# TensorE's slot reordered: transposition of x first, then the maximum, then the row, then projection and output matmuls

## Time and profile before

| what | value |
|---|---|
| median of 3 runs | 469.8 us (468.24 to 472.76) |
| the profiled execution, its own time | 469.28 us |
| its span, first to last instruction | 467.5 us |
| mean granted TensorE clock | 0.937 |
| busy: TensorE, its weight loads | 384.9 us (82%), 338.0 us (72%) |
| busy: VectorE, ScalarE, GpSimd | 380.4 us (81%), 358.4 us (77%), 295.8 us (63%) |

### The profile page before, as it was taken

The page is one execution under the profiler, slowest core; times in us unless marked ns, Lnnn a source line. Parts: engine busy times, 40 slices in busy tenths (PEclk is TensorE's granted clock), DMA queues, the critical chain, the costliest instruction groups (busy, mean ns, idle before and its releaser), DMA issues. The chain is left out here.

```text
span 467.5 us, 9322 instructions
## 1 busy us (share of the span) xinstructions
PE 384.9 (82%) x2825; PEld 338.0 (72%) x2825; DVE 380.4 (81%) x1384; ACT 358.4 (77%) x869; POOL 295.8 (63%) x425
## 2 busy tenths in 40 slices
PE   2799998999677697796787896999999959989870
PEld 2699997998666586686786796989888856555440
DVE  0358889988978899999999864889889897888862
ACT  1577998999857889899889846578778747787864
POOL 4237886777553463553554665677777776878883
PEclk9999999999888988998898889899999998999985
DMA  6999661000000000000000000000000000011112
GB/s 163 226 248 236 150 103 28 2 1 1 2 1 1 1 1 1 2 0 1 2 1 0 3 1 1 1 2 1 1 2 1 2 1 1 19 65 54 68 72 92
DMA packets 8757, 18.21 MB, mean 39 GB/s; under 512 B 1280, under 2 KB 2560, under 8 KB 8704
## 3 DMA queue, kind: packets, MB, share of 16 engines
q0 software_dynamic: 2304, 8.39, 9.6%
q1 hardware_dynamic: 2976, 4.52, 2.9%
q10 hardware_dynamic: 3424, 4.66, 2.9%
HBM read 21.76 MB, written 4.19 MB: 56 GB/s over the span
## 5 line engine op out<-in xcount | busy, mean ns | idle before, releaser
L459 PE MATMUL o_ps<-h_scaled,PT 128*128 128x129 f32 (+1 forms) x1536 | 191.8, 286 | 12.5 <-DVE y L947 9.6
L459 PEld LDWEIGHTS o_ps<-h_scaled,PT 128*128 128x128 f32 x1536 | 186.9, 202 | 13.7 <-issue 10.1
L676 ACT ACTIVATE X<-y,offset,rstd 128x128 f32<-128x128 f32 x256 | 104.7, 480 | 21.4 <-POOL offset L268 21.3
L897 DVE SCALAR_TENSOR_TENSOR PT<-rows_ps,factors,MT 128x512 f32<-128x512 f32 x128 | 88.9, 736 | 0.0
L401 PE MATMUL h_ps<-wx,xT 128*128 128x130 f32 x384 | 69.1, 322 | 3.9 <-DVE smax L863 2.5
L259 POOL TENSOR_TENSOR rstd<-var_eps,neg_half 128x4 f32<-128x4 f32 x64 | 66.0, 1031 | 5.0
L401 PEld LDWEIGHTS h_ps<-wx,xT 128*128 128x128 f32 x384 | 59.0, 219 | 13.5 <-issue 12.1
L967 DVE BATCH_NORM_STATS2 stats<-y 128x6 f32<-128x128 f32 x256 | 55.9, 280 | 6.6
L649 ACT ACTIVATE edge<-edge,col_tmp,col_full 128x512 f32<-128x512 f32 x64 | 48.4, 803 | 14.9 <-DVE edge L875 14.9
L249 POOL TENSOR_TENSOR h_scaled<-hx,col_tmp 128x512 f32<-128x512 f32 x16 | 16.7, 1042 | 56.2 <-DVE col_tmp L915 56.2
L225 POOL TENSOR_TENSOR mean_term<-h_mean,empty_row 128x512 f32<-128x512 f32 x32 | 38.2, 1193 | 18.4 <-DVE residual L947 16.6
(11 more groups left out here) (99 smaller groups left out, 693.4 us busy)
## 6 DMA issues: line engine op xcount, KB each, us to landing
MT<-adj_by_j POOLq DMA_DIRECT2D x16, 512.0 KB, 10.3
X<-x SPq DMA_DIRECT2D x16, 256.0 KB, 6.1
out<-X ACTq DMA_DIRECT2D x16, 256.0 KB, 2.0
w_rel<-w SPq DMA_DIRECT2D x1, 256.0 KB, 5.6
w_back<-w_by_output ACTq DMA_DIRECT2D x1, 192.0 KB, 3.4
wx<-w_by_input ACTq DMA_DIRECT2D x1, 192.0 KB, 5.4
bias<-b ACTq DMA_DIRECT2D x1, 64.0 KB, 4.8
bias<-b SPq DMA_DIRECT2D x1, 64.0 KB, 9.7
```

Of the source, the lines that this page charges most:

```text
L459: last = pe.matmul(o_ps[it.b][:, ic, first:1 + D], PT[:, it.b, jc, ic * P:(ic + 1) * P], h_scaled[:, it.b, jc, first:1 + D], start=(jc == ...
L676: last = act.activation(X[:, g, c, :], y[:, b, c, :], ACT.Identity, bias=offset[:, b, c:c + 1], scale=rstd[:, b, c:c + 1])
L897: dve.scalar_tensor_tensor(out=PT[:, it.b, c, :], in0=rows_ps[:], scalar=factors[:, it.b, 1, c:c + 1], in1=m, op0=ALU.max, op1=ALU.mult, * ...
```

## The change

TensorE's steps of an attention slot come in another order: transposition of n+4, maximum of n+2, rows of n+1, then projection and output matmuls as before. In slot 18, where the flag uses the same PSUM tensor, the transposition stays behind the flag. No instruction and no semaphore is added or taken away; the other engines' lists are the same.

```diff
             def attention_slot(at, n):
+                if at(4) and n != G + 2:
+                    next_transpose(at(4))
+                if at(2):
+                    spread_max(at(2))
                 if at(1):
                     spread_rows(at(1))
-                if at(2):
-                    spread_max(at(2))
                 if n == G + 2:
...
                     pe.wait_ge(sem("flag_max"), 1)
-                if at(4):
                     next_transpose(at(4))
                 if at(3):
                     project(at(3))
```

## The result

The changed kernel takes 487.39 us (median of 4 runs, 484.56 to 489.3) against 470.11 us for the kernel before on the same chip (4 runs, 468.24 to 472.76): ratio 1.0352, 95% interval 1.0319 to 1.0386. The forecast was 476.0 with a range of 470.5 to 481.5. The direction was right; the growth that was forecast, 6.6 us, is less than half of the 17.3 us that came.

The account below looks back on a forecast made before the run. No engine is full; a loop over several engines paces each slot, with VectorE's maximum, TensorE's spreading and VectorE's maximum of that. Terms 6.6 + 0.7 + 1.8 - 2.5 - 1.5 + 1.5 = +6.6 on 469.3 gave 476 us, range 470.5 to 481.5.

Parts of the forecast that it names:

- Step 1: Layer 1, items 19 to 30: row behind xT closes a ScalarE loop, +0.55 us a slot, +6.6 us in all.
- both extras: Layer 1: normalisation waiting for GpSimd's offset (up to 0.33 us) and TensorE's slow restart (up to 0.33); 0.15 a slot together.
- The clock falls: Rival, chance 0.08: restart block at 1.2 GHz in every layer-1 slot, 16.2 us in place of 6.6, total 485.6 us.
- Step 2: Layer 1, items 15 to 17: rows up to 0.6 us later behind five transpositions, +0.7 us (0 to 1.8).
- Step 3: Layer 2, first two slots: L429 0.9 us later behind a transposition that waits for xT, +1.8 us (0.9 to 2.7).
- Step 4: Layer 2, steady: L429 loaded earlier, row moved into smax's time, 0.22 us a slot, -2.5 us (-1.5 to -3).
- Step 5: Layer 0: TensorE saves 0.15 us a slot, but packed ScalarE limits the lead, -1.5 us (0 to -2).
- Step 6: Filling the pipeline: maximum behind four transpositions at the lower clock, an early row late, +1.5 us (0.5 to 2).

Follow-up runs that it names:

- the earlier offset: Changed kernel, with GpSimd computing 1/std and offset of n-2 before the ELU's low part of n-1 in layer 1: 476.66 us; only from slot 20 on, 475.45 us.
- T M R: TensorE order transposition (n+4), maximum (n+2), row (n+1), as in the changed kernel; the kernel before has row, maximum, transposition: 487.39 us against 470.11.

## Why the prediction was wrong: point by point

**Step 1, layer 1: the loop was right, what I laid on top of it was not, and this is the step that failed.** The forecast was +6.6 in this stage, 0.40 a slot bare and 0.15 on top; it came to +17.5. The closed loop of xT, transposition, maximum, row and q_rows is shown three ways: the old order in layer 1 alone brings back 8.58; the row alone ahead of the transposition does the same; and with both extras taken away the slot is 8.94 where the bare sum said 9.00. Of the two extras I had said "each holds in part of the slots" and taken 0.15. In a slot with the slow restart they are 0.98 for the clock and 0.41 for the offset, on a bare loop of 0.34: together 1.73, the measured 10.33 - 8.60. The clock's share is shown by ten added matmuls: 9.35 in place of 10.33, with ScalarE's part unchanged. The offset's share is shown by 8.94 in place of 9.35 between the two kernels with ten added matmuls. So the term of the sum that failed is the extra of 0.15 a slot, which measured 1.39 in slots 24 to 28. Its upper bound was too low even by its own pieces: 0.40 + 0.33 + 0.33 is 1.06 a slot, not 0.90, and the piece for the clock, 0.33, priced the row alone and left the transposition and the maximum in front of it at full speed. The +17.5 also runs over 13 slots, 19 to 31, where 12 were priced.

Two errors lie under the 0.15. My argument against the lower clock was one restart after 2.95 us that ran at full speed, five loads long. One restart was too few to look at. The same trace of the kernel before has three later restarts in the same place, each after a pause of 2.65 us (2.71 us for the one of the earlier trace rows, read on the matmuls), and the slow part begins earlier in each. Of the last two:

```profile
230.70 0.32 PE L429 MATMUL h_ps<-ident,smax_own 128*128 128x128 f32 x1 [2.65 <-DVE smax_own L858]
230.86 0.88 PE L386 MATMUL xT_ps<-ident,X 128*128 128x128 f32 x4
...
248.03 0.98 PE L386 MATMUL xT_ps<-ident,X 128*128 128x128 f32 x4
```

The four transpositions took 0.68 at 196.52, 0.77 at 213.69, then 0.88 and 0.98, where 0.60 is the full speed. So a slow start of this block was in sight before the change. And my own forecast made the slot longer and left TensorE's work the same, so its pause had to grow: the slow restarts of slots 22 to 29 in the changed kernel follow pauses of 3.01 to 3.41 us. Second, I added the extras as independent parts, while they depend on each other. Shown is that the earlier offset shortens slots 19 to 31 by 9.2 us, where 0.41 in each of the thirteen is 5.3, and that q_rows waits less for TensorE there. My account of the way, that the longer slot lengthens the pause, the pause lowers the clock and the slow chain lengthens the slot again, is argued and not shown: the longest pauses, 3.41 us, follow slots at full speed, in which TensorE is done sooner, and equal pauses were followed by slow and by fast restarts.

**The rival *The clock falls* named the larger missing term**, and I gave it 0.08. That its 485.6 lies so close to 487.39 is in part luck: its slow block came in slots 22 and 24 to 29 and not in all twelve, it had nothing for the offset, and the fill, layer 0 and layer 2 came out otherwise than its sum had them. The Trainium skill ("TensorE: Matmul & The Clock Gate", section "Part 4: PE-mode transpose") says that transposes don't count as work for the clock's rise; what it gave, the 485.6, was much nearer than my sum. The trace doesn't settle its reason: after a pause of 2.16 us nine such transposing matmuls ran at full speed, at 219.82 with the earlier offset, and no kernel here replaces them by other matmuls of the same length.

**Step 2, first slots of layer 1:** +0.7 forecast, +0.7 measured. **Step 3, head of layer 2:** +1.8 forecast, +1.8 measured, but the reason is not shown. The order that I priced is there: the transposition's loads, which L429 is now queued behind, wait for xT and are slow besides (weight loads of the changed kernel):

```profile
309.03 0.72 PEld L386 LDWEIGHTS xT_ps<-ident,X 128*128 128x128 f32 x4 [3.39 <-ACT xT L596]
```

Yet the kernel with the same order here and the old one in layer 1 goes through these four slots in 33.74 us, 0.7 *less* than before. So the 1.8 depends on the state in which layer 1 hands over, and that it met my number may be chance. The seam slots 30 and 31, ahead of the four, were 1.1 us longer there, and in another kernel the order of before took 35.88 us for the four slots, 1.4 more than in the kernel before itself; a step of 1.8 can't be told from that. What of it is the order's own stays open.

**Step 4, steady layer 2:** -2.5 forecast, -3.1 measured. The transposition's loads at 324.63, L429's at 325.01, VectorE's wait for it down from the 0.78 of the earlier trace rows to 0.47; a slot is 6.66 in place of 6.97, 0.31 where I had 0.22. (In layer 2, weight loads, then VectorE:)

```profile
324.63 0.42 PEld L386 LDWEIGHTS xT_ps<-ident,X 128*128 128x128 f32 x4
325.01 0.14 PEld L429 LDWEIGHTS h_ps<-ident,smax_own 128*128 128x128 f32 x1
...
325.43 0.29 DVE L864 TENSOR_REDUCE smax<-h_ps 128x1 f32<-128x128 f32 x1 [0.47 <-PE h_ps L429]
```

**Step 5, layer 0:** -1.5 forecast, -3.9 measured. "ScalarE has nothing to give" was wrong. In the earlier trace rows it reads as packed because its shifts starts 0.04 after the accumulator read ends, and also 0.04 after VectorE's smax ends; I took the tie for a bound on ScalarE. In the changed kernel smax is early and ScalarE's slot shows its own length:

```profile
87.56 0.29 DVE L864 TENSOR_REDUCE smax<-h_ps 128x1 f32<-128x128 f32 x1 [0.31 <-PE h_ps L429]
...
88.04 0.29 ACT L611 ACTIVATE shifts<-shift_k,smax 128x3 f32<-128x3 f32 x1
...
94.12 0.29 ACT L611 ACTIVATE shifts<-shift_k,smax 128x3 f32<-128x3 f32 x1
```

94.12 - 88.04 is 6.08, 0.14 less than 6.22, and VectorE's own slot came out at 5.95. ScalarE falls behind by 0.13 a slot, which the slack of 0.7 that I had found carries: shifts starts 0.56 after smax's end in slot 7, the longer slot 8 takes this lag away, and by slot 13 it is 0.50 again. So nearly the whole layer ran at VectorE's 5.95. The orders with the maximum first went further, to 5.79. How long that would hold in a longer layer was not tried.

**Step 6, filling:** +1.5 forecast, +2.4 measured, above its bound of 2. In the six other kernels whose slot 0 has the order T M R its smax starts between 25.35 and 28.89, in the six with another order there between 22.78 and 26.53. The sign holds, but one trace each can't size this step to better than some 2 us. The spread goes with the clock during the fill: its slots take 4.03 us at the full clock and 5.22 to 5.74 at the lower.

So of an error of about 11 us (487.4 for 476.0), step 1 is +10.9, step 6 +0.9, step 3 and step 2 nothing, and steps 4 and 5 give back 3.0; together 8.8. The remaining 2 to 3 us are the height of the timed median over the profiled execution (487.39 for 484.56), which was 0.5 before.

Most of what the prediction named as its signs came: q_rows idle (2.27 for 1.4), the idle piece before the edge exponential gone, TensorE's L386 waiting for xT, L677 waiting for L268, row groups at 1.06 for 0.60. Those with a length missed: slots of 10.33 in layer 1 for 9.0 to 9.3, of 5.95 in layer 0 for 6.2, and item 0's smax 0.6 later for 1.2.

## What to carry to other kernels

In an in-order queue, a step that depends on another engine's *last* piece of a slot makes everything behind it depend on that piece too: trace each of those back to its consumer, and if it is the first piece of the same engine, the loop is closed and its length is the new slot. When such a loop makes the slot longer with the work of TensorE unchanged, compute its new pause, look at every restart of the trace and not at one, and price the whole chain at both clock levels; two additions on a closed loop need not be worth the sum of their own sizes. Which order is best differs by stage: here the row first where ScalarE copies it, the maximum first where VectorE waits for it, which gave 460.11 us against 470.86 for the kernel before.

## What the runs showed of the hardware that I had not expected

- Of the restarts of this block in steady layer 1, those after pauses of up to 2.26 us ran transposition and row at full speed (0.66 and 0.60 us), those after 2.51 and 2.52 us nearly did (0.66 and 0.70), and those after 3.00 to 3.41 us were slow in whole or in part (1.12 and 1.06; 0.96; 0.67 and then 1.06). The head of the block can be fast and its end slow. Pauses between and elsewhere don't fit one order: 0.66 and then 0.98 after 2.44 us, slow from the start after 2.36 us (1.11, the earlier offset, slot 30), and full speed (0.66 and 0.60) after 3.29 us at the head of layer 2 with 20 added matmuls.
- 20 float32 matmuls of 128 columns by 126 came as 40 records of 0.114 us each (4.55 / 40), twice the work that I had counted for the filler.
- Ten matmuls whose result nobody reads made the kernel 10.2 us faster (477.19 for 487.39), since the clock was at 1.00 in place of 0.85 while the loop ran through TensorE.
